# Expert loop of a fused attention and mixture-of-experts layer: the transpose of the next tile's activation is moved in front of the second layer, and the small routing operations behind the bias

## The reference, cut to what matters

```python
logits = xt @ Wg.T
top1 = jnp.argmax(logits, axis=-1)
xhat = (xt - mu) * jax.lax.rsqrt(var + LN_EPS)
def body(y, p):
    s_e, b_e, w1, bb1, w2, bb2, eid = p
    h = jax.nn.gelu((xhat * s_e + b_e) @ w1 + bb1, approximate=False)
    out = h @ w2 + bb2
    mask = (top1 == eid)[:, None].astype(out.dtype)
    return (y + mask * out, None)
...
x = x + y
```

## Time and profile before

| | us |
|---|---|
| time, median of 3 runs | 1605.61 (1605.38 to 1607.28) |
| the profiled execution: its time | 1603.25 |
| the profiled execution: its span | 1601.5 |
| expert loop, from the first matmul of the second layer to the end of the span | 1426.5 to 1601.5 |

### The profile page before, as it was taken

The page is one execution under the profiler, slowest core; times in us unless marked ns, Lnnn a source line. Parts: engine busy times, 40 slices in busy tenths (PEclk is TensorE's granted clock), DMA queues, the critical chain, the costliest instruction groups (busy, mean ns, idle before and its releaser), DMA issues.

```text
span 1601.5 us, 24339 instructions
## 1 busy us (share of the span) xinstructions
PE 1522.3 (95%) x7988; PEld 1259.8 (79%) x7988; DVE 1036.8 (65%) x2496; ACT 714.0 (45%) x2015; POOL 441.9 (28%) x312
## 2 busy tenths in 40 slices
PE   6799999999999999999999999999999999998998
PEld 3688787877778787878787778878787878777886
DVE  5756565575757566565767575757575656657776
ACT  2545354443535353444435353636363544424443
POOL 3512131221122221212211222222222212127776
PEclk8899999999999999999999999999999999999999
DMA  9200101021020201120110201020101011457773
GB/s 228 79 27 1 53 1 53 14 51 52 16 71 14 73 14 67 27 69 15 41 46 21 66 14 60 11 59 1 53 1 53 1 54 53 160 184 265 228 237 112
DMA packets 67735, 105.93 MB, mean 66 GB/s; under 512 B 26966, under 2 KB 35431, under 8 KB 66590
## 3 DMA queue, kind: packets, MB, share of 16 engines
q1 hardware_dynamic: 56814, 70.68, 15.6%
q0 software_dynamic: 10800, 33.70, 5.5%
HBM read 59.47 MB, written 46.72 MB: 66 GB/s over the span
## 4 chain that ended last, share of the span: by engine, by line
PE 59%; DVE 21%; DMA 7%; ACT 6%; issue 4%; POOL 2%; DVEq 0%; POOLq 0%; SPq 0%; ACTq 0%
PE bank L1023 13%; PE bank L885 11%; PE bank L1048 11%; PE bank L1003 6%; PE bank L909 4%; DMA region<-rows,pos 4%; PE bank L1453 4%; PE bank L1497 4%; DVE actH L992 3%; ACT E L941 3%; DMA rows<-in_x 3%; POOL region L1191 2%; DVE xn L843 2%; PE bank L1117 2%; PE bank L1436 2%
## 5 line engine op out<-in xcount | busy, mean ns | idle before, releaser
L1048 PE MATMUL bank<-w,actH 128*128 128x512 f32 x1536 | 373.5, 393 | 2.5 <-DVE actH L1038 2.3
L1023 PE MATMUL bank<-actA,w 128*128 128x512 f32 x1536 | 366.9, 394 | 0.0
L1023 PEld LDWEIGHTS bank<-actA,w 128*128 128x128 f32 x1536 | 286.0, 188 | 62.4
L1048 PEld LDWEIGHTS bank<-w,actH 128*128 128x128 f32 x1536 | 282.5, 188 | 60.4 <-DVE actH L1038 5.9
L968 POOL TENSOR_TENSOR E<-E,rc 128x1232 f32<-128x1232 f32 x64 | 145.1, 2267 | 471.0 <-DVE rc L963 471.0
L1038 DVE TENSOR_TENSOR actH<-htmp,actH 128x512 fp32r<-128x512 f32 x128 | 88.8, 693 | 166.8 <-ACT actH L1034 166.8
L1033 ACT ACTIVATE htmp<-bank,b 128x512 f32<-128x512 f32 x128 | 88.2, 689 | 226.2 <-PE bank L1023 226.2
L885 PE MATMUL bank<-actA,wq 128*128 128x512 f32 x768 | 182.0, 390 | 0.0
L941 ACT ACTIVATE E<-bank,mx 128x77 f32<-128x77 f32 x512 | 157.8, 365 | 45.7 <-DVE mx L918 45.7
L885 PEld LDWEIGHTS bank<-actA,wq 128*128 128x128 f32 x768 | 144.2, 188 | 30.4 <-issue 0.5
L1191 POOL DMA_INDIRECT region<-rows,pos x64 | 63.1, 987 | 376.3 <-DVE pos L1185 337.2
(11 more groups left out here) (165 smaller groups left out, 2019.5 us busy)
## 6 DMA issues: line engine op xcount, KB each, us to landing
rowB<-region SPq DMA_DIRECT2D x71, 258.0 KB, 3.5
rows<-in_x SPq DMA_DIRECT2D x64, 256.0 KB, 3.2
e_raw<-in_E SPq DMA_DIRECT2D x16, 256.0 KB, 2.7
region<-padrow SPq DMA_DIRECT2D x9, 258.0 KB, 3.6
w_raw<-in_W SPq DMA_DIRECT2D x1, 2048.0 KB, 11.1
w_raw<-in_W SPq DMA_DIRECT2D x2, 1024.0 KB, 7.9
e_parts<-e_high SPq DMA_DIRECT2D x8, 256.0 KB, 2.0
e_parts<-e_low SPq DMA_DIRECT2D x8, 256.0 KB, 2.3
```

The costliest lines, as they stand in the source:

```text
L1023: mm = pe.matmul(p[:], w, a, start=k == 0 and j == 0, stop=k == KD - 1 and j == 2)
L1048: mm = pe.matmul(p[:], a, w, start=m == 0 and j == 0, stop=m == MF - 1 and j == 2)
```

## The change

Two tables of the schedule are edited, and no instruction is added or removed. In the expert loop B_G(t+1) now stands in front of B_Y(t). And the drip operations: so far one was emitted behind B_Y and one behind B_H, and now two are emitted behind B_H and none behind B_Y.

```diff
         for t in range(-5, NT):
-            for kind, ahead in (("B_Y", 0), ("B_G", 1), ("B_X", 5), ("B_XT", 4), ("B_H", 3)):
+            for kind, ahead in (("B_G", 1), ("B_Y", 0), ("B_X", 5), ("B_XT", 4), ("B_H", 3)):
                 if 0 <= t + ahead < NT:
                     step(kind, t + ahead)
...
-        DRIP = {"KP": 5, "Q": 2, "PT": 2, "AV": 2, "HLO": 12, "Y": 1, "TT": 1, "B_Y": 1, "B_H": 1}
+        DRIP = {"KP": 5, "Q": 2, "PT": 2, "AV": 2, "HLO": 12, "Y": 1, "TT": 1, "B_H": 2}
```

## The result

The changed kernel takes 1624.41 us (median of 4 runs, 1623.25 to 1625.97) against 1605.49 of the kernel before beside it: ratio 1.0116, 95% interval 1.0099 to 1.0134, so 19 us slower. The forecast was 1620.9, in a range of 1614 to 1628. Its profiled execution takes 1623.9 (forecast 1618.5), with a span of 1622.1.

A forecast was written before the change was run, and what follows sets the result against it. A ring of POOL and DVE, 4.51 us a pair, was taken as the bound. +18.0 - 0.6 - 2.1 = +15.3 gave 1618.5 us for a profiled execution, 1620.9 as median; range 1614 to 1628.

The forecast's parts named there:

- a ring of POOL and DVE: Expert loop: additions, POOL's output, both `b2` and `hb` form a gapless chain, 4.51 us a pair against PE's 4.28.
- Second layer behind the transpose, on PE: Expert loop on PE: waits for `gT` should go; alone worth up to 5 us, if the ring allowed it.
- the later stretch: Tiles 22 to 66, 100.18 us before: 22 pairs at 0.82 more, +18.0 us, bounds +16.5 to +19.8.
- The addition behind `gT`: Expert loop on DVE: the addition queues behind `gT`, which waits for ACT; ring grows from 4.51 to 5.33 us a pair.
- turn: From DVE's `hb` over ACT's GELU and copy to DVE's `gT`; with `gT` to addition 1.08 us, in place of 0.26.
- POOL is first: Later stretch: POOL's `b2` holds DVE off from 2.16 us after the even addition; DVE, ready at 2.32, is late by 0.16.
- the first rival: DVE's `b2` goes first in every pair, PE's 4.28 sets the pace: faster, 1592 to 1598 us; chance 0.06.
- the one of alternating pairs: DVE's `b2` goes first in some pairs, 4.63 to 4.81 us a pair: 1603 to 1610 us; chance 0.12.
- The first part: Tiles 0 to 22: pairs go from 5.48 to 5.33 us, 1 given back for routing: -0.6 us, bounds -6 to +5.
- The drip operations: Behind `hb` two of 0.14 fit into DVE's 0.62 us to spare: no cost; without that cover 0.6 a pair.
- The end: From tile 66 on, where DVE has no `b2`: 8.61 us becomes 6.5, so -2.1 us, bounds -3 and 0.
- Signs in the profile: Later stretch: DVE idle 0.6 us before most `gT`, its `b2` 1.4 us, PE 80% busy, PE's waits moved to L1497.

The follow-up runs named there:

- Kernels 6: Kernel before the change, with every `b2` addition on DVE and none on POOL: 1593.13 us, ratio 0.9919 to the kernel before.
- kernel 7: Changed kernel with POOL's `b2` in front of POOL's output: 1591.93 us, ratio 0.9916 to the kernel before.
- kernel 9: Kernel before the change, with POOL's `b2` in front of POOL's output: 1598.03 us, ratio 0.9952 to the kernel before.
- kernel 3: Changed kernel with its new order on PE and ACT only, DVE's addition again in front of `gT`: 1603.56 us, ratio 0.9985 to the kernel before.
- kernel 8: Changed kernel with ACT's GELU behind its copy of `gT`: 1605.45 us, ratio 0.9998 to the kernel before.
- kernel 11: Changed kernel with GELU behind the copy of `gT` and POOL's `b2` in front of its output: 1592.32 us, ratio 0.9920 to the kernel before.
- 4: Changed kernel with its new order on DVE only, PE's transpose again behind the second layer: 1623.88 us, ratio 1.0123 to the kernel before.
- kernel 10: The changed kernel run again as it is: 1624.91 us, ratio 1.0114 to the kernel before.
- kernel 1: Kernel before with only B_G put before B_Y, drip operations left in place: 1621.60 us, ratio 1.0098 to the kernel before.
- kernel 2: Kernel before with only the drip operations moved, two behind B_H: 1603.05 us, ratio 0.9986 to the kernel before.

## Why the prediction was right, by its own steps

**What bounds the kernel now.** Right, and it carried all else: a ring of POOL and DVE of 4.51, under a PE that looks 99% busy. Kernels 6, 7 and 9 cut the ring in two ways and come out at 4.29 to 4.37, close to the 4.28 taken from PE's shortest distance.

**Second layer behind the transpose, on PE.** This step was wrong, and the sum didn't use it. PE's waits at L1497 should have gone, with a second layer more of lead for `gT`. In kernel 3, the change on PE alone, the lead is not there: L1497 starts 0.27 behind `gT` as before. In the changed kernel it starts 0.25 or 0.71 behind, in turn, and PE waits 6.5 us and its weight load 10.6 at L1497 in the later stretch. A lead of 1.25 in the median is in kernels 8 and 11 only, where GELU stands behind the copy.

**The addition behind `gT`.** Forecast 1.08 for turn and addition, measured 0.88 + 0.21 = 1.09; ring 5.33 forecast, 5.36 measured; +18.0 forecast for the stretch, +18.5 measured. Kernels 3 and 4 show that it is this half, and kernels 7 and 8 that both the ring and the turn are needed for the loss.

**POOL is first.** Right: DVE's `b2` is held in every pair of the later stretch, although its row starts 0.18 before POOL's in most. The reading of one held drip operation decided it, against the reading by the starts of the rows, on which the first rival stood. That rival and the one of alternating pairs did not come true in the changed kernel; in kernel 8, one pair did (below). Two pairs had a lead of 0.46 and 0.49, more than the 0.30 that the reading covered, and were held as well.

**The first part** is the term that was off: -0.6 forecast, +2.9 measured (+1.3 in kernel 10), within its bounds of -6 and +5. I put the new ring in place of the mean of 5.48. But that mean isn't a ring: the matmuls of the last block's logits and the chain behind them are in it as lumps, and they stay. Drip operations were held nearly only from tile 11 on, and between tiles 12 and 22 the forecast holds: 27.84 before, 26.77 and 26.75 in the two traces after. Between tiles 0 and 12 it is 32.63 before, 36.64 and 35.06 after. Tiles 4 to 8 pay the ring's price, 1.2 in both traces; the largest piece is another in each, the 2.9 at tiles 8 to 10 in the first and 1.15 at tiles 10 to 12, with the two held drip operations, in kernel 10.

**The drip operations** cost nothing where two small ones fit into the wait for ACT, as forecast, but not always: kernel 10 has one held for 1.90 at 1463.52 and one for 1.92 at 1467.26 in the new place. The order alone (kernel 1) has 60.02 us in the first part against 61.81 and 63.41 with both edits, so in the new order their move seems to cost 1.8 to 3.4 us, where in the old order it gained 2.3. That is from one trace of each and the difference between two traces of the changed kernel is 1.6, so it stays open.

**The end.** -2.1 forecast, -2.3 measured: POOL's outputs follow one another at 1.29 to 1.31.

**Signs in the profile.** The idle before `gT` and its releaser came as written (0.54 where I had 0.6). PE's waits moved to L1497 only in part: its weight load waits 10.6 us there and 11.8 at L1476. Two numbers there were wrong: DVE's `b2` takes 2.06 and not 1.4, though my own times, ready at 2.32 and `hb` at 4.25, already give 1.9; and PE's busy share is 88% and not 80%, since busy time counts matmuls that are drawn out over a late start, the same effect that I had named for the kernel before.

## What to carry to other kernels

An engine that is 99% busy by the profile need not set the pace: take the distance between two like instructions of successive iterations and look for the closed chain whose durations and hand-overs add up to it without a gap. An edit is priced by what it puts into that chain. Here an addition that stood between a request to another engine and the use of its answer was the cover for that engine's turn; moving it behind cost the whole turn, and the useful edit was one that took an instruction out of the chain, the swap of two instructions on POOL: 7.7 us in the kernel before (kernel 9), 13.5 together with the change (kernel 7), by the ratios.

## What the runs showed of the hardware that I had not expected

A POOL instruction that reads SBUF holds off a DVE instruction whose tensor inputs all lie in SBUF well before its own row begins, if POOL is still in the instruction ahead of it. In the kernels above `b2` rows on DVE start up to 0.56 us ahead of POOL's (in the changed kernel at 1462.12, for 2.42) and a drip operation 0.61 ahead (L1344 in kernel 11 at 1460.13, for 1.94) and are held to POOL's end. Those that start 0.64 or more ahead went through, such as L1271 in the kernel before, 0.65 ahead at 1469.38, in 0.15. Most that were held have two SBUF inputs, but the copy L1267 with one was held too (1.92 in kernel 10 at 1467.26). `hb` and `gT`, which read a product in PSUM, were not held in any kernel: `gT` at 1504.58 takes its 0.28 inside POOL's `b2`. A row that joins two operations misleads here: in kernel 2 the pair of L1271 at 1466.75 starts 0.68 ahead, but its first operation went through and the held one starts at 1466.93, 0.50 ahead. The lead isn't all, though: in kernel 8 a `b2` that started 0.38 ahead went through and POOL's took longer instead, in the one place of its kind:

```profile
1579.18 0.68 DVE L1422 TENSOR_TENSOR rowB<-rowB,b2e 128x512 f32<-128x512 f32 x1
```

```profile
1579.56 1.44 POOL L1422 TENSOR_TENSOR rowB<-rowB,b2e 128x512 f32<-128x512 f32 x1
```

So who is first can't be read off the starts of the rows to within half a microsecond. The Trainium skill ("SBUF — State Buffer", section "Who interferes with whom") has the exclusion, and that the order of issue decides; the traces agree with that if issue is taken to lie ahead of the row, which no row here shows directly.
